# Mixture of experts: the product of the gated half and the up half moves from GpSimd to VectorE

## The reference, cut to what matters

```python
p = softmax(x @ gate_w)                            # 1024 tokens x 64 experts
w = p of the 8 largest, divided by their sum       # 0 for the other experts
for e in range(64):
    g = x @ gate_proj[e]                           # 1024 x 96
    u = x @ up_proj[e]                             # 1024 x 96
    h = silu(g) * u                                # silu(g) = g * 1 / (1 + exp(-g))
    acc += w[:, e] * (h @ down_proj[e])            # 1024 x 256
```

## Time and profile before

| | us |
|---|---|
| median of 3 runs (2714.34 to 2716.99) | 2715.83 |
| the profiled execution | 2715.17 |
| its span in the profile | 2710.7 |
| busy: PE / DVE / ACT / POOL | 2105.0 / 1842.6 / 1343.1 / 552.8 |

### The profile page before, as it was taken

How to read it: one execution, slowest core, us unless ns; L and a number is a source line. 1 busy time by engine, 2 the same in 40 slices (tenths; PEclk the granted TensorE clock), 3 DMA queues, 4 the chain that set the end, 5 groups by cost and what they waited for, 6 DMA issues and landing times. The chain is left out here.

```text
span 2710.7 us, 35502 instructions
## 1 busy us (share of the span) xinstructions
PE 2105.0 (78%) x11529; PEld 1347.3 (50%) x11529; DVE 1842.6 (68%) x3836; ACT 1343.1 (50%) x2543; POOL 552.8 (20%) x648
## 2 busy tenths in 40 slices
PE   4999999965664666485685797476989999946978
PEld 3667676753332333263464254344667666622545
DVE  6878787856998999764686884825435353468834
ACT  5665666646886888434432266421324333341651
POOL 2323233303553554000451000200101010100000
PEclk8999999986666766687687699578999999976989
DMA  4000000002111110220410300050000000013010
GB/s 190 3 1 4 1 3 1 1 11 67 41 35 44 44 42 11 84 79 6 93 31 29 89 3 17 0 201 11 1 2 0 1 0 2 1 45 102 26 33 16
DMA packets 61665, 93.02 MB, mean 34 GB/s; under 512 B 9121, under 2 KB 55793, under 8 KB 58845
## 3 DMA queue, kind: packets, MB, share of 16 engines
q1 hardware_dynamic: 57486, 80.01, 9.6%
q10 hardware_dynamic: 4016, 11.04, 1.1%
HBM read 80.10 MB, written 9.44 MB: 33 GB/s over the span
## 5 line engine op out<-in xcount | busy, mean ns | idle before, releaser
L1245 DVE SCALAR_TENSOR_TENSOR moe_acc<-moee_eo,moee_wt,moe_acc 128x256 f32<-128x256 bf16 x512 | 229.6, 514 | 0.3
L756 DVE SCALAR_TENSOR_TENSOR l_acc<-l_px,l0w_chan,l_acc 128x253 f32<-128x253 f32 (+2 forms) x288 | 137.7, 478 | 98.3 <-POOL l_acc L724 97.7
L1158 POOL TENSOR_TENSOR moee_hb<-moee_gb,moee_ub 96x1024 bf16<-96x1024 bf16 x64 | 146.8, 2294 | 228.0 <-DVE moee_gb L1252 228.0
L1171 PE MATMUL moee_pu<-moe_xb,moee_wb 128*96 128x512 bf16 x256 | 101.4, 538 | 101.6 <-DVE moee_ub L1227 101.6
L1207 ACT CAST moee_eo<-moee_po 128x512 bf16<-128x512 f32 x224 | 115.3, 594 | 80.8 <-PE moee_po L1182 80.8
L1182 PE MATMUL moee_po<-moee_db,moee_hb 96*128 96x256 bf16 x512 | 110.5, 390 | 45.0 <-DVE moee_eo L1236 27.4
L1171 PE MATMUL moee_pg<-moe_xb,moee_wb 128*96 128x512 bf16 x256 | 100.8, 536 | 32.2 <-POOL moee_db L1143 23.6
L1171 PEld LDWEIGHTS moee_pu<-moe_xb,moee_wb 128*96 128x96 bf16 x256 | 35.3, 161 | 165.2 <-DVE moee_ub L1227 142.8
L1182 PEld LDWEIGHTS moee_po<-moee_db,moee_hb 96*128 96x128 bf16 x512 | 65.5, 134 | 102.5 <-POOL moee_hb L1158 76.1
L1655 ACT ACTIVATE l2a_ex<-l2a_pS 128x512 f32<-128x512 f32 x128 | 73.9, 606 | 77.8 <-PE l2a_pS L1568 73.3
L496 PE MATMUL l_pz<-xT,l0w_w_in 128*128 128x256 f32 x384 | 110.5, 411 | 2.4 <-DVE l_sz L795 2.4
(11 more groups left out here) (615 smaller groups left out, 5860.9 us busy)
## 6 DMA issues: line engine op xcount, KB each, us to landing
moee_wf<-in_moe_up SPq DMA_DIRECT2D x64, 192.0 KB, 2.3
l3w_w_in<-in_l_w_in ACTq DMA_DIRECT2D x1, 8224.0 KB, 22.2
m1b_bc<-bc_rows SPq DMA_DIRECT2D x16, 512.0 KB, 6.2
l0w_w_in<-in_l_w_in SPq DMA_DIRECT2D x1, 6448.0 KB
moee_df<-in_moe_down SPq DMA_DIRECT2D x64, 96.0 KB, 2.1
l_qs<-parts_q SPq DMA_DIRECT2D x48, 128.0 KB
l0w_w_out<-in_l_w_out SPq DMA_DIRECT2D x1, 3072.0 KB
parts_q<-l_pieces SPq DMA_DIRECT2D x16, 192.0 KB, 2.3
```

Source lines behind the costliest of these rows:

```text
L756: nc.vector.scalar_tensor_tensor(out=a, in0=px[:, 0:S - (L0_CONV - 1 - c)], scalar=w, in1=a, op0=ALU.mult, op1=ALU.add).then_inc(tap_done, 1)
L1158: nc.gpsimd.tensor_tensor(hb[:, e % 3, :], gb[:, e % 4, :], ub[:, e % 4, :], ALU.mult).then_inc(h_done, 1)
L1171: last = nc.tensor.matmul(ps[0:MOE_F, half, :], wb[:, e % R, k, n * MOE_F:(n + 1) * MOE_F], xb[:, k, half * 512:(half + 1) * 512], start=( ...
L1245: last = nc.vector.scalar_tensor_tensor(out=acc[:, t, :], in0=eo[:, i % 2, t, :], scalar=wt[:, i, t:t + 1], in1=acc[:, t, :], op0=ALU.mult ...
```

## The change

GpSimd's loop keeps only the weight casts; the waits for `gated`, `u_read` and `o_done` and the multiply into `hb` go to VectorE, behind its multiply by the reciprocal, with the same operands.

```diff
                     cast_weights(1)
                     cast_weights(2)
-                    for e in range(U):
-                        if e + 3 < U:
-                            cast_weights(e + 3)
-                        pool.wait_ge(gated, e + 1)
-                        pool.wait_ge(u_read, e + 1)
-                        if e >= 3:
-                            pool.wait_ge(o_done, e - 2)
-                        nc.gpsimd.tensor_tensor(hb[:, e % 3, :], gb[:, e % 4, :], ub[:, e % 4, :],
-                                                ALU.mult).then_inc(h_done, 1)
+                    for e in range(3, U):
+                        cast_weights(e)
...
                             nc.vector.tensor_tensor(gb[:, i % 4, :], gb[:, i % 4, :], ex[:, i % 4, :],
                                                     ALU.mult).then_inc(gated, 1)
+                            dve.wait_ge(gated, i + 1)
+                            dve.wait_ge(u_read, i + 1)
+                            if i >= 3:
+                                dve.wait_ge(o_done, i - 2)
+                            nc.vector.tensor_tensor(hb[:, i % 3, :], gb[:, i % 4, :], ub[:, i % 4, :],
+                                                    ALU.mult).then_inc(h_done, 1)
```

## The result

| | before | changed |
|---|---|---|
| median, us | 2715.09 (4 runs, 2712.8 to 2716.99) | 2683.37 (4 runs, 2679.32 to 2684.82) |
| profiled execution, us | 2715.17 | 2683.46 |
| its span, us | 2710.7 | 2681.7 |
| the experts' stage, us | 475.09 | 444.24 |

The ratio is 0.9891 with a 95% interval of 0.9874 to 0.9907; the median before has one run more than the 2715.83 above. "The experts' stage" is taken from the start of the router's last multiply (L1091) to the start of the addition into `res` behind the mixture (L1264, after the change L1263). It lost 30.85 us, the span 29.0, so the other stages together came out 1.8 longer, and the time around the span 2.7 shorter (4.5 to 1.8), and neither of the two is explained by anything in the change.

What follows compares the result with a forecast made beforehand. VectorE was taken to bound the experts' stage at 7.005 us an expert. Steady part 21.7 and drains 4.6 less, fill 0, made 26.3 off 2715.17, so 2688.9, rounded to 2690 against the median; range 2672 to 2706.

Steps and rivals of the forecast that it cites:

- VectorE's plain sum sets the pace: Experts' stage: VectorE, busy without idle time at 7.005 us an expert, bounds it; its instruction pitches add up to the time.
- The add and clamp stood behind GpSimd's multiply: VectorE's L1230 in each expert: its pitch falls from 1.54 to 0.33 us, minus 1.21 an expert.
- The new multiply and its wait: VectorE, each expert: plus 0.60 us for the moved multiply, plus 0.14 for waiting on the gated half before it.
- The clean expert: VectorE's summed pitches for one expert without cast costs after the change: 6.27 us.
- The casts: GpSimd's weight casts beside VectorE: 0.39 us a pair, bounds 0 and 0.90, for about 25 of 28 experts.
- Drain and fill: Block ends: drain from 18.92 to 16.63 us, 4.6 less over two blocks; block starts: 0, bounds minus and plus 1 us.
- the prediction's steps from the profiled execution to a rounded median: Whole kernel: 2715.17 less 26.3 gives 2688.9; that execution is 0.66 below the median, so 2689.5, rounded to 2690.
- Rival A: Casts fall on PSUM copies or the gap, costing 0 to 0.15 us a pair: 2670 to 2678; chance 0.15.
- B: The loop through TensorE and ScalarE takes over, pitch 6.7 to 7.0 us: 2694 to 2711; chance 0.16.
- C: GpSimd's casts stop VectorE wholly at the gated multiply and the new one: 2715 to 2734; chance 0.07.
- D: The add and clamp stays at 1.54 us because something else holds it: 77 us more, 2767; chance 0.02.

Runs made afterwards that it cites:

- E1: Changed kernel, but GpSimd also does a multiply of the old size at the old moment into a spare tile; 2734.02 us, 1.0076 of the kernel before.
- E3: Changed kernel, but after a block's first six experts GpSimd casts only 2 elements per partition of each weight tile; 2665.35 us, 0.9841 of the kernel before.
- E5: Changed kernel, with GpSimd's cast pairs also waiting until VectorE's new multiply ends and its PSUM copy begins; 2665.84 us, 0.9820 of the kernel before.
- E6: Changed kernel, with VectorE's PSUM copy of the next up half put between its two multiplies; 2657.91 us, 0.9799 of the kernel before.
- E7: Changed kernel, with ScalarE making all four copies of every po and VectorE none; 2660.43 us, 0.9800 of the kernel before.
- E2: Changed kernel without the multiply by the up half on any engine; 2632.11 us, 0.9716 of the kernel before.

## Why the prediction was right

*VectorE's plain sum sets the pace.* Shown: 196.15 us for 28 experts became 182.2 with VectorE still without idle time, E1 put time back on VectorE and the pitch grew, and what E3, E5, E6 and E7 took off VectorE's sum came off the pitch (E7: 0.30 and 0.305).

*The add and clamp stood behind GpSimd's multiply.* Shown by the removal (1510 to 420 ns) and by E1, which brings it back with data that nobody reads. The predicted 1.21 us came out as 1.54 - 0.33 = 1.21.

*The new multiply and its wait.* 0.60 and 0.14 were predicted; measured clean, 0.61 and 0.11 (a pitch of 0.71 for L1245). The clean expert was 6.255 against 6.27.

*The casts.* This term was mis-sized. The prediction put 0.39 a pair, the price among accumulations; the 28 experts took 182.2 - 28 x 6.255 = 7.1 us more than clean, 0.28 over 25 pairs. The price among accumulations was right (0.40), but more than every second pair runs only at the two multiplies and costs 0.19, since its second half goes under the PSUM copy. Over both blocks that is 5.3 us of the difference.

The reading of the Trainium skill (SBUF — State Buffer, Who interferes with whom) by which a pair costs its whole 0.90 isn't borne out: E3 shows 14.8 us for the 52 pairs that it cut short, 0.28 each. What the Trainium skill says there of who interferes, work with two SBUF inputs, fits E5, where the casts under the PSUM copy cost nothing. Two inputs aren't the whole of it, though: the add and clamp has one SBUF input, and GpSimd held it too (E1, and for 0.07 us in E5).

*Drain and fill.* Drain: 16.81 against 16.63 predicted, 2.1 saved in each block instead of 2.3. Fill: put at 0; the first block's was unchanged (21.7), the second's 1.2 longer (20.93 to 22.12, from the last accumulation to the first L1229), 0.3 of it a later first load. The rest wasn't traced to its cause; in that fill TensorE's gate matmuls of the second expert took 1.91 us (from 862.16) instead of 1.03 (from 875.14 before).

Together 2 x 13.9 + 4.2 - 1.2 = 30.8 in the stage, against 26.3 predicted: 5.3 more by the casts and 0.8 by the clean expert, 1.6 less by drain and fill. The rest of the distance from 2690 to 2683.4, about 2, is the time around the span and the other stages (0.9) and the prediction's steps from the profiled execution to a rounded median (1.1). Rival A (the casts miss, 0 to 0.15 a pair) was near the truth for more than half of the pairs, at 0.19; B, C and D are refuted by E2, by the stage's length, and by the 420 ns.

## What to carry to other kernels

Where VectorE is the pace, read not only what it does but how long the same instruction takes when GpSimd is idle: a mean of 1510 ns beside a shortest record of 412 is a stall that no list of waits shows. Moving work from GpSimd to a saturated VectorE can gain, if the work costs less there than the stall that it caused (here 0.74 against 1.21). What GpSimd must still do is best released when VectorE begins an instruction with a PSUM source, and dependent VectorE instructions are best kept apart by an independent one (E5 and E6); then look at once for the engine behind (here ScalarE at 5.95).

## What the runs showed of the hardware that was not expected

A waiting GpSimd cast doesn't always get in between two VectorE instructions. In the changed kernel some of those released among the accumulations got in within 0.2 us and cost 0.40 a pair (773.64, 0.66 us long). Others stood open until the gap of 0.04 us between the two multiplies: the cast of 762.18 ends at 763.57, where L1245 ends at 763.20 and L1251 starts at 763.24. E6 takes that gap away, and there a cast stood open for 2.82 us until the PSUM copy; the mean record of the weight cast is 1820 ns (640 to 1000 us). So the gap accounts for the pairs at 0.19. Why some casts get in among the accumulations of the changed kernel, and the one at 739.91 in E6, released 1.39 us into them like the one at 773.64, does not, was not settled.

TensorE's granted clock in the 28 experts rose from 0.64 to 0.77 with the shorter pitch, without any change in its work. VectorE, which sets the pace, waited for TensorE only in the fills (19.2 us before, 19.3 after).
